# State-space stage of a fused block: y collected with its tokens on the partitions, and work moved between the engines

## The reference, cut to what matters

```
xn     = layernorm(x)
x_ssm, z = split(xn @ W_in.T)                   # 512 channels each
xc     = silu(causal_conv4(x_ssm))
dt_raw, B, C = split(xc @ W_x.T)                # 1, 16 and 16 columns
dt     = softplus(dt_raw * dt_w + dt_b)         # per token and channel
h[t,:,n] = exp(dt*A[:,n]) * h[t-1,:,n] + dt * B[t,n] * xc[t]      # 16 states n
y[t]   = sum over n of h[t,:,n] * C[t,n]  +  xc[t] * D
x      = x + (y * silu(z)) @ W_out.T
```

## Time and profile before

| | |
|---|---|
| time, median of 3 runs | 3475.97 us (3469.48 to 3479.46) |
| the profiled execution: its own time | 3468.01 us |
| its span (first to last instruction) | 3466.5 us |
| mean granted TensorE clock | 0.929 of full speed |
| state-space stage | 0 to about 1084 us |
| projections for attention | to about 1330 us |
| attention | to about 2775 us |
| experts | the rest |

### The profile page before, as it was taken

The page is one execution under the profiler, slowest core; times in us unless marked ns, Lnnn a source line. Parts: engine busy times, 40 slices in busy tenths (PEclk is TensorE's granted clock), DMA queues, the critical chain, the costliest instruction groups (busy, mean ns, idle before and its releaser), DMA issues. The chain is left out here.

```text
span 3466.5 us, 45186 instructions
## 1 busy us (share of the span) xinstructions
PE 2918.8 (84%) x12864; PEld 1118.6 (32%) x12865; DVE 2463.6 (71%) x2786; ACT 1864.7 (54%) x3378; POOL 1016.7 (29%) x548
## 2 busy tenths in 40 slices
PE   5799899889775848999999999999999963999990
PEld 1234334443333511222222222222222252566650
DVE  0699999999995678888887888888888065111113
ACT  3556665665542305777676767777677810222220
POOL 2778778877860210000000000000000036100007
PEclk8999999999988958999999999999999975999995
DMA  1111111111112420111111110001110036111114
GB/s 41 43 47 55 40 50 55 46 43 46 49 40 70 163 86 13 31 32 32 32 32 33 32 29 22 26 22 30 32 32 19 1 115 242 48 44 45 44 38 145
DMA packets 114924, 177.08 MB, mean 51 GB/s; under 512 B 26128, under 2 KB 73872, under 8 KB 114704
## 3 DMA queue, kind: packets, MB, share of 16 engines
q1 hardware_dynamic: 100880, 134.54, 12.9%
q0 software_dynamic: 13824, 39.86, 3.5%
HBM read 129.63 MB, written 44.43 MB: 50 GB/s over the span
## 5 line engine op out<-in xcount | busy, mean ns | idle before, releaser
L1427 DVE TENSOR_REDUCE nmh<-ring 128x2 f32<-128x1024 f32 x1024 | 1186.8, 1218 | 211.0 <-PE ring L1319 210.0
L1303 ACT ACTIVATE prob<-s_ps 128x512 f32<-128x512 f32 x2048 | 1065.2, 603 | 473.9 <-PE s_ps L1344 472.1
L767 DVE TENSOR_TENSOR_SCAN h<-dA,state,bx 128x512 f32<-128x512 f32 x512 | 617.8, 1262 | 119.0 <-ACT dA L606 119.0
L391 POOL TENSOR_TENSOR bx<-u,bb 128x2048 f32<-128x2048 f32 x128 | 578.7, 4525 | 197.2 <-DVE h L767 197.0
L1344 PE MATMUL s_ps<-qs,ks 98*128 98x512 bf16 x2048 | 599.8, 388 | 23.8 <-issue 14.1
L1356 PE MATMUL acc<-prob,vst 128*32 128x512 f32 x4096 | 552.7, 612 | 1.0 <-ACT prob L1303 0.7
L606 ACT ACTIVATE dA<-dt,aneg 128x512 f32<-128x512 f32 x512 | 348.8, 691 | 270.0 <-DVE h L767 269.9
L673 PE MATMUL y_ps<-h,ident 128*128 128x512 f32 x1024 | 478.5, 611 | 1.1 <-DVE h L774 1.1
L1319 PE MATMUL ring<-k,q 64*128 64x512 bf16 x2048 | 380.1, 404 | 104.1 <-DVE nmh L1427 36.3
L1291 POOL COPY vst<-v_all 128x544 f32 (+1 forms) x16 | 10.2, 641 | 1362.4 <-PE acc L1356 1362.4
L1344 PEld LDWEIGHTS s_ps<-qs,ks 98*128 98x128 bf16 x2048 | 153.2, 97 | 519.2 <-ACT prob L1303 415.0
(11 more groups left out here) (218 smaller groups left out, 2456.4 us busy)
## 6 DMA issues: line engine op xcount, KB each, us to landing
bb<-b_rows SPq DMA_DIRECT2D x128, 256.0 KB, 3.1
parts<-part POOLq DMA_DIRECT2D x48, 256.0 KB, 2.8
qs<-parts SPq DMA_DIRECT2D x192, 64.0 KB, 2.2
ks<-parts SPq DMA_DIRECT2D x192, 64.0 KB, 2.2
xt<-slots_in POOLq DMA_DIRECT2D x72, 128.0 KB, 2.3
slots_out<-yt SPq DMA_DIRECT2D x72, 128.0 KB, 1.7
q<-parts SPq DMA_DIRECT2D x128, 64.0 KB, 2.1
k<-parts SPq DMA_DIRECT2D x128, 64.0 KB, 2.1
```

What stands on the lines that cost most here:

```text
L391: nc.gpsimd.tensor_tensor(bx[:, n % BR], u[:, b], bb[:, n % RB, None, :].to_broadcast([P, KI, CH]), ALU.mult).then_inc(s_bx, 1)
L767: nc.vector.tensor_tensor_scan(h[:, n % HR, d, :], dA[:, d % 2, :], bx[:, n % BR, d, :], state[:, b, n, d:d + 1], ALU.mult, ALU.add).then_ ...
L1303: nc.scalar.activation(prob[:, k % PR, j, :], s_ps[:, m % SR, :], ACT.Exp, scale=SC).then_inc(s_exp, 1)
L1427: nc.vector.tensor_reduce(nmh[:, :, t, at], ring[:, s, :, :], AX.X, ALU.max, negate=True).then_inc(s_free[s], 1)
```

## The change

1. **y is gathered turned.** `collect` now takes h*C of 128 channels x 128 tokens as the weights and the identity as the moving operand, in transpose mode, and adds into `y_ps`: 16 transposes of 128x128 where there were four matmuls of 128x512. `y_ps` has tokens on the partitions, channels along the free dimension. `skip_part` (xc * D) is turned in the same way.
2. z is projected straight into that layout (`project_z`). After `gate` the product must go back to channels on the partitions for W_out: `gated` transposes it block by block into `fill`, and `take_g` (ScalarE) writes it back into `zs`. That is four more uses of `fill` a chunk (EACH 18 to 22).
3. **GpSimd multiplies block 3 of every even state index by C** (`times_c` on GpSimd: 128x512, both inputs in SBUF), behind `bx(n)` for state n-4. VectorE then multiplies three blocks (128x1536) in even states and four in odd ones. The row of C comes by DMA (`load_c`, from a new DRAM table `c_rows`; two buffers), and TensorE's `collect` of an even state waits for GpSimd (`s_hp`) ahead of block 3.
4. **ScalarE normalises the input** (`normalize`, four times 128x256, n = 7 and 8) and GpSimd's `norm_apply` goes; VectorE computes -mean/std for it (`mean_part`, n = 4).
5. **TensorE adds the residual**: an identity matmul of x opens each accumulation in `project_out`; VectorE's `residual` becomes a copy on ScalarE (`take_o`).
6. Places in the order: `second_part` moves from step 6 to step 7, behind `softplus_minus`; `take_z` to steps 9 to 11, the input transposes to 11, W_in to 12 and 13, the convolution to 14 (two), 15 and 0, 1 of the next chunk.

Cut to its core:

```diff
-        y_ps = ps("y_ps", [P, KI, CH])
+        cc = sb("cc", [P, RC, CH])
+        y_ps = ps("y_ps", [P, TT, DI])
...
+            def load_c(i, b, n):
+                c, k = 2 * i + b, n // SHARE
+                wait_apart(sp, s_prst, 32 * (c + 1), s_w)
+                wait_apart(sp, s_hp, NP * c + k - RC + 1, s_w)
+                sp.dma_start(cc[:, k % RC, :], c_dram[b, n:n + 1, :].partition_broadcast(P)
+                             ).then_inc(s_c[k % RC], 16)
...
+            def times_c(c, n):
+                k = n // SHARE
+                wait(pool, s_c[k % RC], 16 * ((NP // RC) * c + k // RC + 1))
+                wait(pool, s_sv, NS * c + n + 1)
+                nc.gpsimd.tensor_tensor(h[:, n % HR, KI - 1, :], h[:, n % HR, KI - 1, :], cc[:, k % RC, :], ALU.mult
+                                        ).then_inc(s_hp, 1)
...
+                    if n % SHARE == 0 and n >= BR:
+                        times_c(c, n - BR)
+                    elif n % SHARE == 0 and has_prev:
+                        times_c(c - 1, n - BR + NS)
                     if n == 6 and has_next:
                         rest(c + 1, 1 - b)
-                    if n == 8 and has_two(i):
-                        norm_apply(c + 2)
...
+            def normalize(c, t):
+                wait(act, s_mr, c + 1)
+                last = nc.scalar.activation(xn[:, t, :], xn[:, t, :], ACT.Identity, bias=mr[:, t:t + 1],
+                                            scale=rs[:, t:t + 1])
...
+            def take_g(c, b, d):
+                wait(act, s_full, fill_G(c, d) + 1)
+                nc.scalar.copy(turned(b, d), fill[:, :].rearrange("p (t q) -> p t q", t=TT)).then_inc(s_free, 1)
...
+                if n in (5, 6) and has_prev:
+                    take_g(c - 1, 1 - b, 2 * n - 10)
                 if n == 5 and has_next:
                     softplus_exp(c + 1)
                 if n == 6 and has_next:
                     softplus_plus(c + 1)
-                    second_part(c + 1, 1 - b)
                 if n == 7 and has_next:
                     softplus_minus(c + 1)
-                    take_z(c + 1, 1 - b, 0)
+                    second_part(c + 1, 1 - b)
+                if n in (7, 8) and two:
+                    normalize(c + 2, 2 * n - 14)
+                    normalize(c + 2, 2 * n - 13)
...
+            def collect(c, n):
                 for d in range(KI):
-                    last = nc.tensor.matmul(y_ps[:, d, :], ident[:, :], h[:, n % HR, d, :],
-                                            start=False, stop=(n == NS - 1))
+                    if n % SHARE == 0 and d == KI - 1:
+                        wait(pe, s_hp, NP * c + n // SHARE + 1)
+                    for t in range(TT):
+                        last = nc.tensor.matmul(y_ps[:, t, d * P:(d + 1) * P], h[:, n % HR, d, t * P:(t + 1) * P],
+                                                ident[:, :], is_transpose=True, start=False,
+                                                stop=(n == NS - 1 and d == KI - 1))
                 last.then_inc(s_ys, 1)
...
                 if n in (5, 6) and has_prev:
-                    project_out(c - 1, 1 - b, n - 5)
-                if n in (7, 8) and has_next:
-                    project_in(c + 1, KI + 2 * n - 14)
-                    project_in(c + 1, KI + 2 * n - 13)
+                    gated(c - 1, 1 - b, 2 * n - 10)
+                    gated(c - 1, 1 - b, 2 * n - 9)
+                if n in (7, 8) and has_prev:
+                    project_out(c - 1, 1 - b, n - 7)
+                if n in (9, 10) and has_next:
+                    project_z(c + 1, 2 * n - 18)
+                    project_z(c + 1, 2 * n - 17)
                 if two:
-                    if n == 9:
+                    if n == 11:
                         transposes(c + 2, 0)
                         transposes(c + 2, 1)
-                    if n in (10, 11):
-                        project_in(c + 2, 2 * n - 20)
-                        project_in(c + 2, 2 * n - 19)
-                    if n in (12, 13, 14):
-                        convolve(c + 2, n - 12)
+                    if n in (12, 13):
+                        project_in(c + 2, 2 * n - 24)
+                        project_in(c + 2, 2 * n - 23)
+                    if n == 14:
+                        convolve(c + 2, 0)
+                        convolve(c + 2, 1)
+                    if n == 15:
+                        convolve(c + 2, 2)
...
+                mine = KI - 1 if n % SHARE == 0 else KI
+                nc.vector.tensor_tensor(h[:, n % HR, 0:mine], h[:, n % HR, 0:mine],
+                                        c_ps[:, None, :].to_broadcast([P, mine, CH]), ALU.mult
```

More of the change, by code:

```diff
@@ L63, in ssm_stage @@
     RB = 4
+    RC = 2
+    SHARE = 2
+    NP = NS // SHARE
     NR = NS + 1
@@ L168, in ssm_stage @@
         s_hc = sem("s_hc")
+        s_hp = sem("s_hp")
+        s_c = [sem(f"s_c{k}") for k in range(RC)]
         s_ys = sem("s_ys")
@@ L409, in _ @@
             every_chunk(pool, prologue, chunk)
+            for n in range(NS - BR, NS):
+                if n % SHARE == 0:
+                    times_c(NC - 1, n)
         @block.scalar
@@ L524, in prologue @@
                 second_part(0, 0)
+                for t in range(TT):
+                    normalize(1, t)
                 for d in range(KI):
@@ L532, in prologue, with between @@
                     take_conv_in(1, d)
-                for d in range(KI - 1):
+                for d in range(KI - 2):
                     take_conv(1, 1, d)
                 act.wait_ge(s_an, 1)
-            def between(i, b, n, has_next):
+            def between(i, b, n, has_prev, has_next):
                 c = 2 * i + b
                 two = has_two(i)
+                if n == 0 and has_next:
+                    take_conv(c + 1, 1 - b, 2)
                 if n == 1 and has_next:
@@ L607, in chunk @@
                                              scale=aneg[:, d, n:n + 1]).then_inc(s_da, 1)
-                    side(i, b, n, has_next)
+                    side(i, b, n, has_prev, has_next)
             every_chunk(act, prologue, chunk)
             save_state(NC - 1, 1, NS - 1)
+            for d, bank in enumerate(end_banks):
+                wait(act, s_full, fill_G(NC - 1, d) + 1)
+                nc.scalar.copy(turned(1, d), bank.rearrange("p (t q) -> p t q", t=TT)).then_inc(s_free, 1)
+            for half in range(2):
+                take_o(NC - 1, half)
         @block.tensor
@@ L628, in project_in, with project_z, turn_back, gated @@
                 last.then_inc(s_full, 1)
+            def project_z(c, t):
+                wait(pe, s_free, fill_Z(c, t))
+                for k in range(KM):
+                    last = nc.tensor.matmul(fill[:, :], xT[:, k, t * P:(t + 1) * P], w_in[:, k, DI:2 * DI],
+                                            start=(k == 0), stop=(k == KM - 1))
+                last.then_inc(s_full, 1)
+            def turn_back(bank, b, d):
+                for t in range(TT):
+                    last = nc.tensor.transpose(bank[:, t * P:(t + 1) * P], zs[:, b, t, d * P:(d + 1) * P], ident[:, :])
+                return last
+            def gated(c, b, d):
+                wait(pe, s_free, fill_G(c, d))
+                turn_back(fill[:, :], b, d).then_inc(s_full, 1)
             def convolve(c, d):
@@ L753, in norm_stats, with mean_part @@
                 last.then_inc(s_mv, 1)
[L755 to L759 removed]
+            def mean_part(c):
+                wait(dve, s_rs, c + 1)
+                nc.vector.scalar_tensor_tensor(mr[:, :], mv[:, :, 0], -1.0, rs[:, :], ALU.mult, ALU.mult
+                                               ).then_inc(s_mr, 1)
             def scans(c, b, n, half):
@@ L784, in prologue @@
                 norm_stats(0)
+                mean_part(0)
                 dve.wait_ge(s_id, 2)
@@ L814, in chunk @@
                         times_c(c - 1, 1 - b, NS - 1)
-                    if n in (6, 7) and has_prev:
-                        residual(c - 1, n - 6)
                     scans(c, b, n, 1)
@@ L819, in chunk @@
                         norm_stats(c + 2)
+                    if n == 4 and has_two(i):
+                        mean_part(c + 2)
             every_chunk(dve, prologue, chunk)
@@ L823, in _ @@
             gate(NC - 1, 1)
-            for half in range(2):
-                residual(NC - 1, half)
 NH = 16
```

147 lines of the change are left out of this document (78 added, 69 removed).

## The result

The changed kernel takes 3543.88 us (median of 4 runs, 3538.42 to 3548.38), the kernel before beside it 3472.72 (4 runs, 3468.06 to 3479.46). The ratio is 1.0203, interval 1.0187 to 1.0219: slower by 71 us. Forecast were 3526 and 3465 to 3590. A second job gave 3544.0 against 3474.81, ratio 1.0204 (1.0187 to 1.0221).

What follows compares the result with a forecast made beforehand. VectorE was taken as the bound, TensorE close behind. Six chunks +59, chunk 6 +2, chunk 7 -6, start 0, end +3 sum to +58 on 3468.0: 3526 us, range 3465 to 3590.

Steps and rivals of the forecast that it cites:

- The chain from T6: Middle chunk: late second_part delays GpSimd's queue, then TensorE's collect(10), then VectorE's times_c(12); 125.9 us against 120.2, +5.7.
- T6: Start of step 7 in a chunk, where step 6's scans on VectorE have ended; zero point of the predicted times.
- the clock's 1.7: First W_in product behind TensorE's idle before collect(10) runs at half clock: 1.7 us more a chunk, bounds 0 and 5.2.
- step 14's 2.4: Step 14: two convolutions, a spread and a collect overfill TensorE, 10 us in a 6.5 us step; 2.4, bounds 0 and 3.5.
- my own mark of a wrong forecast: Middle chunk: forecast is wrong if collect waits for GpSimd nowhere, or GpSimd pauses again by step 13.
- start and chunk 0: Before the loop 0, give or take 3 us; chunk 0 pays a middle chunk's +9.8, between 5.7 and 14.4.
- chunk 6: Has no W_in products; times_c(12) about 5 us later than before, less 3.3 saved: +2 us.
- chunk 7: Last chunk, prepares nothing, so GpSimd keeps up: -6 us.
- behind it: After the loop: last collect -1.7, transposes and four copies back +3.4, residual at low clock +1.7: +3 us.
- the ring of four absorbs it: Faster rival: GpSimd's lateness at collect(10) is absorbed and VectorE's own saving shows, -39 us (3429); chance 0.16.
- The even rival: Only second_part is in time, so GpSimd's chain starts earlier; chunk +1.4, in all +7 us, 3475; chance 0.08.
- The clock as a bound: Much slower rival: TensorE at half clock throughout gives 3760 us, for half of the work 3600; chance 0.10.

Runs made afterwards that it cites:

- table of four: Changed kernel with GpSimd's share and second_part in step 7 taken back singly and together; ratios to the kernel before: change 1.0203, second_part back 1.0073, no share 0.9954, both 0.9931.
- both edits undone: Changed kernel without GpSimd's multiplication by C and with second_part back in step 6: 3452.84 us, ratio 0.9931; in a later job 3439.04, 0.9929.

## Why the prediction was right, and where it was off

**The bound and its replacement** (right). VectorE was the bound; now a chain over GpSimd, TensorE and ScalarE is. The table of four shows it: the loss comes with the share and grows with the late second part.

**VectorE's own saving** (right). Predicted -5.25 a chunk; busy 115.7 became 110.6, -5.1. The multiplication of three blocks takes 1740 ns in its group, as worked out. `mean_part` takes 0.14. I had set aside a rule of the Trainium skill (SBUF - State Buffer, SBUF: two separate sides) by which it could wait for a `bx`; its row in the chunk shown starts at 676.83, as the scans ahead of it end, and GpSimd's next `bx` at 676.99, behind it, as I had argued. The two never ran together, so the rule was not tested, and there was nothing to add.

**Single costs.** A `collect` of 16 at full clock: 1.7 predicted, 1.74 measured (618.19 - 616.45). GpSimd's multiplication: 1.13 predicted, 1.27 measured (1269 ns in 64), 0.14 too little, from a row with 17 partitions. GpSimd's sum 101 predicted, 101.1 measured. ScalarE +5 predicted, 74.6 to 78.9 measured. TensorE: 81 us of work predicted, 97.4 busy in the row; part of that is time at half clock, and how much wasn't parted.

**The chain from T6** (right, nearly to the number):

| | predicted | chunk shown |
|---|---|---|
| `rest_of_rest` starts | T6 + 6.3 | 6.3 |
| `times_c(10)` on GpSimd ends | T6 + 50.8 | 51.1 |
| VectorE's `times_c(12)` starts (with the clock's 1.7) | T6 + 58.0 | 58.9 |
| from there to the next T6 (with step 14's 2.4) | 72.0 | 72.8 (2.1 of it step 14, 2.1 "issue") |
| the chunk | 130.0 | 131.7 (five: 130.4 on average) |

The first W_in product behind the wait took 3.56 for 1.88, which are the 1.7 I took. That the row from there to the next T6 is met so closely is in part luck: behind step 14 VectorE waited 1.13 and 1.01, for 2.4 predicted, but then came a wait of 2.08 that I had not:

```profile
639.15 2.46 DVE L857 TENSOR_TENSOR_SCAN h<-dA,state,bx 128x512 f32<-128x512 f32 x2 [2.08 <-issue]
```

No other middle chunk has it; profiled again it stands at the same place (2.26), and its cause stays open. Three of the five chunks take 129.5 to 129.7 us. The other one of 131.7 goes with the clock: both of its products behind `collect(10)` ran at half speed (3.62 and 3.73 us). Other details were off: TensorE stood idle 4.64 us ahead of block 3 of `collect(10)` and not 8, since `collect(8)` had held it up already; `collect(6)` waits too (5.64 us), since `times_c(6)` stands behind `bx(10)`, the first of the late queue; the z products run at half clock as well, which is free, because GpSimd is later still; and GpSimd pauses by 1.74 us in step 13, so my own mark of a wrong forecast, a pause by step 13, was met while the chain held. It was a step too strict: 44.5 us of queue, two `bx` and a multiplication are some 55 (564.80 to 619.80), not 60.

**The sum.**

| term | predicted | measured | measured again |
|---|---|---|---|
| start and chunk 0 | 0 + 9.8 | +19.2 | +13.3 |
| chunks 1 to 5 | 5 x 9.8 = 49 | +51.4 | +51.1 |
| chunk 6 | +2 | +4.2 | +3.2 |
| chunk 7 | -6 | -7.2 | -7.4 |
| behind it | +3 | +2.5 | +5.3 |
| sum | +58 | +70 | +65.5 |

The term that was mis-sized most is the first. I gave chunk 0 the price of a middle chunk. From its first scan to the first gate the changed kernel took 141.2 us (116.40 to 257.64) against 124.6 (113.84 to 238.46), +16.6, and +15.3 when both were profiled again; with both edits undone that stretch is 124.0, so it goes with the share and the second part. In three pieces, as after less before, each beside that of the middle chunk shown (from the gates at 516.75 and 477.87 on):

| | chunk 0 | middle chunk |
|---|---|---|
| up to T6 | +1.0 | -2.8 |
| T6 to `times_c(12)` | +13.8 | +11.6 |
| from there to the gate | +1.8 | +2.6 |

Ahead of T6 a middle chunk gains by the change (three shorter multiplications, a residual and an old wait less); chunk 0 has the shorter multiplications, but no residual to lose, and VectorE waits 2.01 us in its first step, which it did not before. And GpSimd's `times_c(10)` ends T6 + 51.1 in chunk 0 too, but there both W_in products ran at half speed (3.62 and 3.78 us) ahead of VectorE's multiplication:

```profile
228.06 1.75 DVE L865 TENSOR_TENSOR h<-h,c_ps 128x1536 f32<-128x1536 f32 x1 [1.18 <-PE c_ps L726]
```

When profiled again only the first of them did. The other 2.6 of the 19.2 lie ahead of the first scan, where one kernel also differs from itself: the changed one began its first scan at 110.25 us when profiled again, 6 earlier. The text also named 112 to 114 us for the last chunk, which contradicts its own -6 on 113; the chunk took 105.9.

**The rivals.** That the ring of four absorbs it fell with the waits. It was a matter of places though: with six states shared, three of them others, the mechanism of that rival holds, and the time is 3419. The even rival holds as a mechanism (the second part in time: `times_c(10)` at T6 + 44.3) but its price, 7 us, was 18 too small, ten of them in chunk 0. Its sum also kept the +2 of a late chunk 6, which in that kernel was 2.1 us shorter than before (116.65 against 118.78). The clock as a bound fell: with all transposes and no share, a chunk takes 116 us at a granted clock of 0.88, less than before at 0.96. The clock is a follow-up cost behind a wait: at `collect(10)` 1 to 2 us in four of the six chunks, and some 3.5 in the two where both products ran slow. In the last chunk, where TensorE does little but transposes, it does stay low (0.73 from 1032 to 1138 us; 0.89 in the last chunk before):

```profile
1050.31 0.51 PE L726 MATMUL c_ps<-c_parts,sel 96*128 96x512 bf16 x1 [4.23 <-DVE h L865]
1050.61 3.50 PE L754 MATMUL y_ps<-ident,h 128*128 128x128 f32 x16
```

The engine had waited 4.23 us for VectorE ahead of the spread, and the `collect` shows 3.50 where one at full clock shows 1.91, in a step with room for it. The Trainium skill (TensorE: Matmul & The Clock Gate, Part 4: PE-mode transpose) says that transposes do not count as activity that brings the clock up. This stretch fits that, but it would look the same from the waits alone, and no run here parts the two.

## What to carry to other kernels

Work given to an engine that is only 80% busy is not free if the engine has a fixed queue with a stretch in which it runs late: first find the steps in which it waits for others, and place the work there, or at least ahead of the longer operation in its queue. Six small multiplications a chunk where the engine had time were worth -20 us, eight that partly fell into its late stretch +49; and those same eight, only moved ahead of the longer operation, cost 33 us less. And where an engine that nobody waited for gets a first consumer, follow its queue from its latest input to that consumer: one wait that was free until then, here a cast moved by a step, gets a price at that moment.

## What the runs showed of the hardware that was not expected

Some 10 to 12 us of waiting in the router, put down to "remote" in the profile, comes and goes between jobs for one and the same program (7.0 in one, 17.4 in another, for the kernel with both edits undone). Two single profiled executions can differ by several us far from any edit (99.6 and 107.3 us over the same eight copies); the ratio from runs of one job did not move (1.0203 and 1.0204).
